# Delta mixer: turning the inverse back by blocks on VectorE instead of by TensorE transposes and ScalarE copies

## The chip, the cores and the metric

The kernel runs on one core of a Trainium2 chip. What counts is the device time of one execution in microseconds. Matrix products run on TensorE (PE in the profile, PEld its weight loads), elementwise work on VectorE (DVE), ScalarE (ACT) and GpSimd (POOL). Each engine works through its own list of instructions in order, and they are held together by semaphores.

## The reference

Four layers work on 2048 rows of 512 features, each adding to its input: a decay mixer, a feed-forward layer, the delta mixer and a second feed-forward layer. The change lies in the delta mixer alone. Its core, cut short:

```python
qkvz = hidden_states @ w_qkvz.T                     # 8 key heads, 16 value heads of 128
yc = silu(conv(q, k, v, 4 taps))                    # causal, per feature
beta, g = sigmoid(b), -exp(A_log) * softplus(a + dt_bias)
def step(S, xs):                                    # over the tokens
    qt, kt, vt, gt, bt = xs
    S = S * exp(gt)[..., None, None]
    delta = (vt - einsum('bhk,bhkv->bhv', kt, S)) * bt[..., None]
    S = S + einsum('bhk,bhv->bhkv', kt, delta)
    return S, einsum('bhk,bhkv->bhv', qt * scale, S)
out = (rmsnorm(o * silu(z)) * norm_weight) @ w_out.T
```

## The kernel before

The recurrence is computed in chunks of 128 tokens. Within a chunk the deltas solve a unit triangular system, and the kernel forms the inverse of its 128x128 matrix explicitly. There are 2 sequences of 8 chunks, 8 key heads and 2 value heads for each key head. One step handles one chunk of both sequences for one key head, so it has U = 4 matrices side by side, in tiles of 128 partitions x 4 x 128. Two such steps, the flights A and B, are worked on interleaved; together they are a pair. For each of 8 heads there are 4 pairs, so `pair` runs 32 times, most of it in hardware loops. Each engine has its own `pair`, which writes out by hand the order of its calls.

**The inverse.** `Tt` holds the transpose of the inverse, `T` the inverse itself, `At` the transposed matrix with its decays and signs. `unit_diagonal` on GpSimd presets `Tt` with the identity, and VectorE's `matrices` (L1586 to 1598) computes `At` and copies its 1-wide off-diagonal entries into `Tt` (L1597). Six levels i = 0 to 5 (`LV` = 6) then join diagonal blocks of 2, 4, ... 64 to blocks of twice the size. Before level i, `Tt` is nonzero only within diagonal blocks of 2, 4, 8, 16, 32 and 64 columns. In each level:

- `turn_back` (TensorE, L1825) transposes the four matrices of `Tt` into the PSUM bank `left`; at the last level only the upper left 64x64 of each.
- `turned` (ScalarE, L1322) copies what is needed of it into `T` (L1328, L1330, L1332).
- `level_x` (TensorE, L1838, "product x" below) multiplies `At` by `T` into `wide`; `level` (ScalarE, L1334) copies half of the result into `X` (L1339).
- `level_y` (TensorE, L1850, "product y") multiplies `X` by `Tt` into `right`; `level` (VectorE, L1600) copies the new blocks into `Tt` with a predicated copy (L1607), at the last level a plain one (L1604).

TensorE's f32 products of 128x128 are recorded as two instructions for each matrix, so one product x or y is x8.

**What lies between.** TensorE's order (L1925 to 1984) puts other products among the levels: `v` and `qk` (parts of the q, k, v projections of later pairs, `project`, L1782), `z` (halves of the z projection, L1795), `from_state` (L1869), `solve` (L1876). In the loop over levels one round is turn A, half a z, product y of B, product x of A, turn B, half a z, product y of A, product x of B; a half-step below is half of that. VectorE's order (L1678 to 1691) puts the convolutions of the next pair (`convolve`, L1526) behind the level copies, one or two behind each, and `right_side` (L1614) behind B's last predicated copy. ScalarE also squares the keys (`tokens`, L1311), which TensorE's `products` (L1821) waits for, and applies the first convolution taps. GpSimd splits the inputs of the pair after next in high and low parts (`split_x`, L1143 and 1147), once in four pairs the weights of the next head too (`low_weights`, L1158), and copies the input of the z projection (`plain_x`, L1153) when the last z is done.

**Semaphores.** `T` counts VectorE's writes of `Tt` (one for the start and one for each level), `Tps` the turns, `T0` the finished `T`, `px` and `py` the products, `X` the copies. `level_x` waits for `T0`, `turn_back` for `T` and at level 0 for `pt`.

Of the kernel before, what the change touches and what calls it, by code (L numbers as in the profile page):

```python
# [6 lines left out]
P = 128  # L7
# [959 lines left out]
def delta_mixer(nc, psum, consts, x_in, x_out, w):  # L967
# [21 lines left out]
    with ExitStack() as ctx:  # L989
# [43 lines left out]
        class Flight:  # L1033

            def __init__(self, g):
                self.i = g
                self.wide, self.left, self.right = bank[2 + 3 * g:5 + 3 * g]

                def buf(n, shape=(P, U, P)):
                    return sb(f"{n}{g}", list(shape))  # L1040

                self.here = slice(g * P, (g + 1) * P)
                self.qkv = buf("qkv", (P, 4, BATCH, P))
                self.z_raw, self.z_act = buf("z_raw"), buf("z_act")
                self.cur = buf("cur", (P, 5, U))
                (self.sr, self.ss, self.rr, self.brk, self.ncc, self.nr, self.rqs, self.q2, self.dcc, self.ssq, self.ssq_q,
                 self.ssq_eps, self.rn, self.rnq) = (
                    buf(n, (P, U)) for n in ("sr", "ss", "rr", "brk", "ncc", "nr", "rqs", "q2", "dcc", "ssq", "ssq_q",
                                             "ssq_eps", "rn", "rnq"))
                self.em, self.em_i = buf("em"), buf("em_i")  # L1050
                self.k_tok, self.rhs = buf("k_tok", (P, BATCH, P)), buf("rhs")
                self.d_end, self.At, self.Pt = (buf(n) for n in ("d_end", "At", "Pt"))
                self.d, self.junk = self.At, self.d_end
                self.T, self.Tt = buf("T"), buf("Tt")
                self.X, self.qs, self.o = self.em, self.T, self.T

                self.xf, self.xn, self.xnT = self.rhs, self.em, self.em_i
                self.s = {n: sem(f"{n}{g}") for n in (
                    "cur", "silu", "zact", "ss", "sse", "rr", "scal", "gU", "dt", "em", "emm",
                    "ktok", "vtok", "ktoks", "vtoks", "kqs", "qss", "at", "atm", "pt", "T0", "diag",  # L1060
                    "T", "Tps", "px", "X", "py", "rhs", "pd", "d", "pod", "dend", "ps", "o", "xf", "sqs",
                    "ssq", "sse2", "rn", "rnq", "xn", "txn", "xnT", "po", "acc")}

        flights = A, B = Flight(0), Flight(1)
# [2 lines left out]
            return b[:, :, :].rearrange("p u t -> p (u t)")  # L1067

        HP = P // 2

        def half(t, level, second):

# [165 lines left out]
        def _(act):  # L1238
# [80 lines left out]
                    act.activation(f.rhs[:, u, :], f.right[:, u, :], ACT.Copy, scale=f.nr[:, u // 2:u // 2 + 1]  # L1319
                                   ).then_inc(f.s["vtoks"], 1)  # L1320

            def turned(f, m, i):  # L1322
                act.wait_ge(f.s["Tps"], LV * m + i + 1)
                if i == 0:
                    act.wait_ge(f.s["xf"], m)
                act.wait_ge(f.s["px"], LV * m + i)
                if i == 0:
                    act.copy(f.T[:, :, :], f.left[:, :, :]).then_inc(f.s["T0"], 1)  # L1328
                elif i < LV - 1:
                    act.copy(half(f.T, i + 1, 0), half(f.left, i + 1, 0)).then_inc(f.s["T0"], 1)  # L1330
                else:
                    act.copy(f.T[0:HP, :, 0:HP], f.left[0:HP, :, 0:HP]).then_inc(f.s["T0"], 1)  # L1332

            def level(f, m, i):  # L1334
                act.wait_ge(f.s["px"], LV * m + i + 1)
                act.wait_ge(f.s["py"], LV * m + i)
# [34 lines left out]
            def pair(h, mm, first=False, start=False, over=False, turn=False, last=False, ahead=True):  # L1371
                m = h * PAIRS + mm
                decay(A, m)
                if not first:
                    output_T(B, m - 1)
                tokens(A, m)
                silu_qkv(B, m)
                silu_z(B, m)
                decay(B, m)
                values(A, m)  # L1380
                tokens(B, m)
                turned(A, m, 0)
                if not last:
                    copy_raw(2, m + 1)
                level(A, m, 0)
                if not last:
                    first_tap(0, m + 1)
                values(B, m)
                turned(A, m, 1)
                level(A, m, 1)  # L1390
                if not last:
                    first_tap(1, m + 1)
                turned(B, m, 0)
                level(B, m, 0)
                for i in range(2, LV):
                    turned(A, m, i)
                    if i == 2 and not last:
                        copy_raw(3, m + 1)
                        if over:
                            high_weights(h + 1)  # L1400
                    level(A, m, i)
                    turned(B, m, i - 1)
                    if 2 <= i <= 3 and not last:
                        first_tap(i, m + 1)
                    level(B, m, i - 1)
                    if i == 4 and not last:
                        copy_z(A, m + 1)
                from_state(A, m)
                turned(B, m, LV - 1)
                if not last:  # L1410
                    copy_z(B, m + 1)
                level(B, m, LV - 1)
                solved(A, m)
                if not last:
                    silu_qkv(A, m + 1)
                    silu_z(A, m + 1)
                mean_square(A, m)
                from_state(B, m)
                if ahead:
                    copy_raw(0, m + 2)  # L1420
                solved(B, m)
                output_T(A, m)
                mean_square(B, m)
                if ahead:
                    copy_raw(1, m + 2)
# [27 lines left out]
        def _(dve):  # L1453
# [132 lines left out]
            def matrices(f, m):  # L1586
                dve.wait_ge(f.s["em"], m + 1)
                dve.wait_ge(f.s["at"], m + 1)
                dve.wait_ge(f.s["scal"], NS * m + 4)
                dve.wait_ge(f.s["px"], LV * m)  # L1590
                for u in range(U):
                    dve.scalar_tensor_tensor(f.At[:, u, :], f.left[:, 2 * (u // 2) + 1, :], f.ncc[:, u:u + 1],
                                             f.em[:, u, :], ALU.mult, ALU.mult).then_inc(f.s["atm"], 1)
                dve.wait_ge(f.s["atm"], U * (m + 1))
                dve.wait_ge(f.s["diag"], m + 1)
                dve.sem_inc(s["dve_gate"], 1)
                dve.copy_predicated(half(f.Tt, 0, 1), first_part[:, :].rearrange("p (a n) -> p a n", n=1),  # L1597
                                    half(f.At, 0, 1)).then_inc(f.s["T"], 1)

            def level(f, m, i):  # L1600
                dve.wait_ge(f.s["py"], LV * m + i + 1)
                dve.wait_ge(f.s["T"], TN * m + 1 + i)
                if i == LV - 1:
                    dve.tensor_copy(f.Tt[0:HP, :, HP:P], f.right[0:HP, :, HP:P]).then_inc(f.s["T"], 1)  # L1604
                    return
                dve.sem_inc(s["dve_gate"], 1)
                dve.copy_predicated(half(f.Tt, i + 1, 1), new_part[:, i, :].rearrange("p (a n) -> p a n", n=LEVELS[i + 1]),  # L1607
                                    half(f.right, i + 1, 1)).then_inc(f.s["T"], 1)

            def right_side(f, m):  # L1610
                dve.wait_ge(f.s["kqs"], m + 1)
# [133 lines left out]
        def _(pe):  # L1745
# [76 lines left out]
                                   start=True, stop=True)  # L1822
                mm.then_inc(f.s["at"], 1)

            def turn_back(f, m, i):  # L1825
                if i == 0:
                    pe.wait_ge(f.s["pt"], m + 1)
                pe.wait_ge(f.s["T"], TN * m + 1 + i)
                if i == LV - 1:
                    pe.sem_inc(s["pe_gate"], 1)  # L1830
                for u in range(U):
                    if i < LV - 1:
                        mm = pe.transpose(f.left[:, u, :], f.Tt[:, u, :], ident[:, :])  # L1833
                    else:
                        mm = pe.transpose(f.left[0:HP, u, 0:HP], f.Tt[0:HP, u, 0:HP], ident[0:HP, 0:HP])
                mm.then_inc(f.s["Tps"], 1)

            def level_x(f, m, i):  # L1838
                pe.wait_ge(f.s["T0"], LV * m + i + 1)
                if i == LV - 1:  # L1840
# [68 lines left out]
            def pair(h, mm, first=False, start=False, over=False, turn=False, last=False, ahead=True):  # L1909
# [23 lines left out]
                decays(B, m)  # L1933
                tokens(B, m)
                v(0, HIGH)
                turn_back(A, m, 0)
                products(B, m)
                level_x(A, m, 0)
                v(1, [0])
                level_y(A, m, 0)  # L1940
                v(1, [1])
                turn_back(A, m, 1)
                v(1, [2])
                level_x(A, m, 1)
                v(1, [3])
                turn_back(B, m, 0)
                level_y(A, m, 1)
                level_x(B, m, 0)
                for i in range(2, LV):
                    f, b = flights[(i - 2) // 2], i % 2  # L1950
                    turn_back(A, m, i)
                    z(f, b, LOW)
                    level_y(B, m, i - 2)
                    level_x(A, m, i)
                    turn_back(B, m, i - 1)
                    z(f, b, HIGH)
                    level_y(A, m, i)
                    level_x(B, m, i - 1)
# [2 lines left out]
                from_state(A, m)  # L1961
                level_y(B, m, LV - 2)
                qk(0, 0)
                turn_back(B, m, LV - 1)
                qk(0, 1)
                solve(A, m)
                level_x(B, m, LV - 1)
# [114 lines left out]
```

## Time and profile before

| | |
|---|---|
| median of 3 runs | 3911.65 us (3900.70 to 3918.11) |
| span of the profiled execution | 3912.5 us (the page gives no other time of it) |
| mean granted TensorE clock | 0.973 |
| TensorE busy | 3615.0 us, 92% |
| VectorE busy | 2131.4 us, 54% |
| ScalarE busy | 1672.4 us, 43% |
| GpSimd busy | 827.5 us, 21% |

The profile is one execution, recorded by instruction. Busy times are shares over four layers with different limits, so a stage has to be looked at by itself. A row of the timeline gives start, duration, engine, line, what is written and read and how many instructions were merged, and in brackets how long the engine had been idle and what released it. A product's duration runs to its modelled end, past the start of the next one, since TensorE works them as a pipeline; what one occupies in the list is the distance to the next start.

### The profile page before, as it was taken

To read this page: it belongs to the slowest core of one execution; us is meant where nothing else is said; L and a number is where in the kernel's file an instruction comes from. 1 tells how busy PE (TensorE), PEld (TensorE's weight loads), DVE (VectorE), ACT (ScalarE), POOL (GpSimd) and SP (SyncE) were. 2 spreads that over 40 slices of the span, in tenths; PEclk is the share of its full clock that TensorE was granted. 3 is DMA by queue.
4 is the path that set the end of the run, shared out by engine and by line. 5 is a ranking of instruction groups with operands and counts; after the bars stand their busy time and mean duration, and the time that the engine had idled before them with its cause. 6 is when DMAs were issued, how large, how long until landed. Compare 5 with 4: busy or idle time off the path is not lost. (4 is left out here: it accounts for less than half of the span.)

```text
span 3912.5 us, 56006 instructions
## 1 busy us (share of the span) xinstructions
PE 3615.0 (92%) x19318; PEld 2817.6 (72%) x19318; DVE 2131.4 (54%) x4279; ACT 1672.4 (43%) x3964; POOL 827.5 (21%) x569
## 2 busy tenths in 40 slices
PE   5996999996899999999999999999999996899998
PEld 2444787884677878778778787787787875787787
DVE  6673555554555555555555555555555553455454
ACT  3343223221455455554554555545555453323221
POOL 1123002000423223223232232232222211201200
PEclk8998999998999999999999999999999998899999
DMA  4003102103000000000000000000000001211110
GB/s 157 11 32 119 43 32 97 65 22 105 11 1 7 17 2 7 17 2 7 18 1 7 18 1 6 18 6 2 18 7 6 12 12 55 76 64 65 65 54 33
DMA packets 61152, 126.88 MB, mean 32 GB/s; under 512 B 3008, under 2 KB 8384, under 8 KB 59840
## 3 DMA queue, kind: packets, MB, share of 16 engines
q1 hardware_dynamic: 60864, 123.26, 9.0%
q8 instruction: 154, 2.52, 0.3%
q14 instruction: 134, 1.10, 0.1%
HBM read 98.09 MB, written 25.17 MB: 32 GB/s over the span
## 5 line engine op out<-in xcount | busy, mean ns | idle before, releaser
L1607 DVE COPY_PREDICATED b_Tt<-b_new_part,banks 128x256 f32<-128x256 uint8 x320 | 157.6, 493 | 557.8 <-PE banks L1858 557.8
L895 PE MATMUL banks<-f_x_hi,f_w_hi 128*128 128x512 f32 x1024 | 408.4, 399 | 43.1 <-ACT f_silu L764 23.7
L895 PE MATMUL banks<-f_x_lo,f_w_hi 128*128 128x512 f32 x1024 | 406.0, 397 | 0.0
L895 PE MATMUL banks<-f_x_hi,f_w_lo 128*128 128x512 f32 x1024 | 405.8, 396 | 0.0
L1526 DVE SCALAR_TENSOR_TENSOR b_conv<-b_raw,b_taps,b_conv 128x512 f32<-128x512 f32 x384 | 376.2, 999 | 2.9 <-ACT b_conv L1279 2.6
L1339 ACT COPY b_em<-banks 128x256 f32<-128x256 f32 x320 | 120.5, 376 | 545.0 <-PE banks L1844 545.0
L1858 PEld LDWEIGHTS banks<-b_Tt,b_em 128*128 128x128 f32 x2560 | 331.5, 192 | 23.9 <-issue 9.6
L1844 PE MATMUL banks<-b_T,b_At 128*128 128x128 f32 x2560 | 347.5, 279 | 0.5 <-ACT b_T L1330 0.5
L1858 PE MATMUL banks<-b_Tt,b_em 128*128 128x128 f32 x2560 | 341.4, 276 | 0.9 <-ACT b_em L1339 0.6
L830 DVE TENSOR_TENSOR f_h<-banks,f_silu 128x512 f32<-128x512 f32 x128 | 87.1, 689 | 435.6 <-PE banks L895 358.8
L1844 PEld LDWEIGHTS banks<-b_T,b_At 128*128 128x128 f32 x2560 | 313.4, 193 | 14.7 <-ACT b_T L1330 7.0
L1795 PE MATMUL banks<-b_w_z,b_x_cur 128*128 128x256 f32 x1024 | 265.4, 383 | 0.0
L895 PEld LDWEIGHTS banks<-f_x_hi,f_w_hi 128*128 128x128 f32 x1024 | 196.9, 192 | 90.8 <-ACT f_silu L764 26.3
L1782 PE MATMUL banks<-b_x_hi,b_w_hi 128*128 128x512 f32 x512 | 253.0, 494 | 9.0 <-POOL b_w_lo L1158 6.0
L1906 PE MATMUL banks<-b_o_cur,b_em_i 128*128 128x512 f32 x512 | 239.7, 612 | 20.5 <-ACT b_em_i L1368 17.6
L1833 PE MATMUL banks<-b_ident,b_Tt 128*128 128x128 f32 x1280 | 203.6, 282 | 35.3 <-DVE b_Tt L1597 16.5
L895 PEld LDWEIGHTS banks<-f_x_hi,f_w_lo 128*128 128x128 f32 x1024 | 196.8, 192 | 42.2
L895 PEld LDWEIGHTS banks<-f_x_lo,f_w_hi 128*128 128x128 f32 x1024 | 197.0, 192 | 41.5
L764 ACT ACTIVATE f_silu<-banks 128x512 f32<-128x512 f32 x128 | 76.2, 597 | 323.8 <-PE banks L895 323.8
L925 PE MATMUL banks<-f_w_hi,f_k_hi 128*128 128x512 f32 x512 | 204.8, 400 | 6.6 <-DVE f_k_lo L852 6.6
L1782 PE MATMUL banks<-b_x_hi,b_w_lo 128*128 128x512 f32 x512 | 203.9, 398 | 0.0
L925 PE MATMUL banks<-f_w_hi,f_k_lo 128*128 128x512 f32 x512 | 203.2, 397 | 0.0
(264 smaller groups left out, 7229.2 us busy)
## 6 DMA issues: line engine op xcount, KB each, us to landing
f_x_tok<-rows SPq DMA_DIRECT2D x16, 1024.0 KB, 7.5
f_stage<-in_ffn_gate SPq DMA_DIRECT2D x8, 1024.0 KB, 6.8
f_stage<-in_ffn_up SPq DMA_DIRECT2D x8, 1024.0 KB, 8.5
f_stage<-in_ffn_down SPq DMA_DIRECT2D x8, 1024.0 KB, 4.9
f_x_res<-rows SPq DMA_DIRECT2D x8, 1024.0 KB, 5.6
f_part<-f_x_res SPq DMA_DIRECT2D x8, 1024.0 KB, 4.3
f_x_res<-f_part SPq DMA_DIRECT2D x8, 1024.0 KB, 5.6
b_w_load<-in_b_qkvz SPq DMA_DIRECT2D x8, 1024.0 KB, 6.1
```

Of the source, the lines that this page charges most:

```text
L830: dve.tensor_tensor(h[:, r, :], up_ps[:, r % 2, :], silu[:, r % 2, :], ALU.mult).then_inc(s_h, 1)
L895: mm = pe.matmul(bank, w[:, b, kind, cols], x[:, k, :], start=(k == 0 and i == 0), stop=(k == KD - 1 and i == 2))
L925: mm = pe.matmul(out_ps[i // 2][:, i % 2, :], k[:, r, toks], w[:, b, DOWN, r * D:(r + 1) * D], start=(b == 0 and r == 0 and j == 0), stop= ...
L1339: act.copy(half(f.X, i + 1, 0), half(f.wide, i + 1, 0)).then_inc(f.s["X"], 1)
L1526: dve.scalar_tensor_tensor(conv[:, i, :, :], raw[:, i, :, tap:tap + 2 * P], taps[:, i, tap:tap + 1], conv[:, i, :, :], ALU.mult, ALU.add). ...
L1607: dve.copy_predicated(half(f.Tt, i + 1, 1), new_part[:, i, :].rearrange("p (a n) -> p a n", n=LEVELS[i + 1]), half(f.right, i + 1, 1)).the ...
L1782: mm = pe.matmul(flat(bank[i % 2]), wt[:, k, i * P:(i + 1) * P], xt[:, k, :, :].rearrange("p b t -> p (b t)"), start=(k == 0 and wt is w_h ...
L1795: mm = pe.matmul(bank[f.i][:, 2 * b:2 * b + 2, :], x_cur[:, k, b, f.here], w_z[:, k, :], start=(k == 0), stop=(k == KD - 1))
L1833: mm = pe.transpose(f.left[:, u, :], f.Tt[:, u, :], ident[:, :])
L1844: mm = pe.matmul(f.wide[:, u, :], f.At[:, u, :], f.T[:, u, :], start=True, stop=True)
L1858: mm = pe.matmul(f.right[:, u, :], f.X[:, u, :], f.Tt[:, u, :], start=True, stop=True)
L1906: mm = pe.matmul(out, f.xnT[:, 2 * b + i, :], o_cur[:, i, :], start=(i == 0), stop=(i == 1))
```

## The change

`T` is no longer made by TensorE and ScalarE. VectorE transposes `Tt` into `T` with its own transpose, which turns each 32x32 block in its place; up to blocks of 32 that is the whole transpose, as all nonzero entries lie within diagonal blocks. At the last level the one new 32x32 block of the upper left 64x64 is transposed to its mirrored place, while the rest of `T` stands from the level before. The transpose follows at once behind the copy that it reads, in `matrices` and in `level`, and signals `T0`. `turn_back`, ScalarE's `turned` and the semaphore `Tps` are dropped, the order of all other calls is kept.

```diff
 # VectorE, behind the first copy in matrices
+                turned(f, m, 0)
+
+            def turned(f, m, i):
+                dve.wait_ge(f.s["T"], TN * m + 1 + i)
+                if i < LV - 1:
+                    dve.transpose(flat(f.T), flat(f.Tt)).then_inc(f.s["T0"], 1)
+                else:
+                    dve.transpose(f.T[QP:HP, :, 0:QP], f.Tt[0:QP, :, QP:HP]).then_inc(f.s["T0"], 1)
 # VectorE, at the end of level (not at the last level)
                 dve.copy_predicated(half(f.Tt, i + 1, 1), new_part[:, i, :]..., half(f.right, i + 1, 1)).then_inc(f.s["T"], 1)
+                turned(f, m, i + 1)
 # ScalarE
-            def turned(f, m, i):
-                act.wait_ge(f.s["Tps"], LV * m + i + 1)
...
-                if i == 0:
-                    act.copy(f.T[:, :, :], f.left[:, :, :]).then_inc(f.s["T0"], 1)
-                elif i < LV - 1:
-                    act.copy(half(f.T, i + 1, 0), half(f.left, i + 1, 0)).then_inc(f.s["T0"], 1)
-                else:
-                    act.copy(f.T[0:HP, :, 0:HP], f.left[0:HP, :, 0:HP]).then_inc(f.s["T0"], 1)
 # TensorE
-            def turn_back(f, m, i):
...
-                for u in range(U):
-                    if i < LV - 1:
-                        mm = pe.transpose(f.left[:, u, :], f.Tt[:, u, :], ident[:, :])
-                    else:
-                        mm = pe.transpose(f.left[0:HP, u, 0:HP], f.Tt[0:HP, u, 0:HP], ident[0:HP, 0:HP])
-                mm.then_inc(f.s["Tps"], 1)
 # TensorE, in pair (six such calls for each flight go, and six of ScalarE's)
                 for i in range(2, LV):
-                    turn_back(A, m, i)
                     z(f, b, LOW)
                     level_y(B, m, i - 2)
                     level_x(A, m, i)
-                    turn_back(B, m, i - 1)
                     z(f, b, HIGH)
                     level_y(A, m, i)
                     level_x(B, m, i - 1)
```

`HP` is 64, `QP` 32, `TN` 7.

## Rows read from the trace of the kernel before

**Rows 1.** Windows view, one pair: busy us of PE, PEld, DVE, ACT, POOL; then PEclk

```profile
2248.66:2318.99 70.33, 68.44 (x430) 54.98 (x429) 38.75 (x91) 37.17 (x105) 17.71 (x15) 1.00 0.00 1
```

**Rows 2.** The line that starts an inverse: its instructions (min/median/max ns)

```profile
L1597 DVE COPY_PREDICATED b_Tt<-b_first_part,b_At x64: 731/743/1164, 1039.4 to 3248.0; 128x256 f32<-128x256 uint8 x64
```

**Rows 3.** Groups by line: count, busy us, mean ns, idle before and its releasers

```profile
L1833 PE MATMUL banks<-b_ident,b_Tt 128*128 128x128 f32 x1280 | 203.6, 282 | 35.3 <-DVE b_Tt L1597 16.5 <-DVE b_Tt L1607 11.4
...
L1835 PE MATMUL banks<-b_ident,b_Tt 64*64 64x64 f32 x256 | 25.2, 218 | 3.6 <-DVE b_Tt L1607 1.5
...
L1339 ACT COPY b_em<-banks 128x256 f32<-128x256 f32 x320 | 120.5, 376 | 545.0 <-PE banks L1844 545.0
```

**Rows 4.** Timeline of TensorE in the levels of that pair (start us, duration us)

```profile
2266.91 0.66 PE L1833 MATMUL banks<-b_ident,b_Tt 128*128 128x128 f32 x4
...
2267.40 1.03 PE L1795 MATMUL banks<-b_w_z,b_x_cur 128*128 128x256 f32 x4
2268.26 1.05 PE L1858 MATMUL banks<-b_Tt,b_em 128*128 128x128 f32 x8
2269.15 1.06 PE L1844 MATMUL banks<-b_T,b_At 128*128 128x128 f32 x8
...
2270.05 0.60 PE L1833 MATMUL banks<-b_ident,b_Tt 128*128 128x128 f32 x4
```

**Rows 5.** Groups by line: VectorE on 128x512 f32, one and two SBUF sources

```profile
L1474 DVE TENSOR_SCALAR b_x_cur<-b_acc,b_mean,b_rstd 128x512 f32<-128x512 f32 x16 | 7.7, 542 | 15.8 <-PE banks L1753 12.7 <-POOL b_rstd L1137 3.1
...
L1654 DVE TENSOR_TENSOR b_em<-b_rhs,b_rnq 128x512 f32<-128x512 f32 x64 | 44.2, 691 | 2.2
```

**Rows 6.** Timeline, start of the inverses of that pair, all engines

```profile
2248.66 1.13 DVE L1597 COPY_PREDICATED b_Tt<-b_first_part,b_At 128x256 f32<-128x256 uint8 x1 [0.18 <-DVE b_At L1592]
...
2249.85 0.66 PE L1833 MATMUL banks<-b_ident,b_Tt 128*128 128x128 f32 x4 [0.47 <-DVE b_Tt L1597]
2249.89 0.27 ACT L1311 ACTIVATION_READ_ACCUMULATOR b_d_end<-banks 128x1 f32 x1
...
2250.34 1.07 PE L1821 MATMUL banks<-b_qkv 128*128 128x256 f32 x4
...
2252.90 1.13 PE L1858 MATMUL banks<-b_Tt,b_em 128*128 128x128 f32 x8
...
2254.29 0.73 DVE L1607 COPY_PREDICATED b_Tt<-b_new_part,banks 128x256 f32<-128x256 uint8 x1 [2.02 <-PE banks L1858]
...
2256.75 0.74 DVE L1597 COPY_PREDICATED b_Tt<-b_first_part,b_At 128x256 f32<-128x256 uint8 x1 [0.19 <-DVE b_At L1592]
...
2259.21 1.10 PE L1844 MATMUL banks<-b_T,b_At 128*128 128x128 f32 x8
```

**Rows 7.** Timeline, VectorE and GpSimd in the middle of that pair's levels

```profile
2260.28 5.68 POOL L1147 TENSOR_TENSOR b_x_lo<-b_xT,b_x_hi 128x512 fp32r<-128x512 f32 x4 [0.18 <-POOL b_x_hi L1143]
...
2263.24 3.27 DVE L1526 SCALAR_TENSOR_TENSOR b_conv<-b_raw,b_taps,b_conv 128x512 f32<-128x512 f32 x2
...
2266.76 0.74 DVE L1526 SCALAR_TENSOR_TENSOR b_conv<-b_raw,b_taps,b_conv 128x512 f32<-128x512 f32 x1
```

**Rows 8.** Timeline, end of the inverses of that pair, all engines

```profile
2284.17 1.89 POOL L1153 COPY b_x_cur<-b_xT 128x2048 f32<-128x2048 f32 x1 [18.21 <-PE banks L1795]
...
2285.53 1.89 PE L1869 MATMUL banks<-b_state,b_qkv 128*128 128x256 f32 x8
...
2288.49 0.45 DVE L1607 COPY_PREDICATED b_Tt<-b_new_part,banks 128x256 f32<-128x256 uint8 x1 [1.89 <-PE banks L1858]
...
2288.83 1.12 DVE L1614 SCALAR_TENSOR_TENSOR b_rhs<-banks,b_cur,b_rhs 128x128 f32<-128x128 f32 x4
...
2290.20 1.05 PE L1876 MATMUL banks<-b_rhs,b_Tt 128*128 128x128 f32 x8
```

**Rows 9.** First pair: granted clock in a stretch (PEclk), and TensorE's timeline

```profile
1040.00:1050.00 10.00, 8.15 (x41) 6.78 (x42) 4.22 (x15) 5.43 (x21) 2.08 (x2) 0.83 0.01 2
...
1042.21 1.72 PE L1821 MATMUL banks<-b_qkv 128*128 128x256 f32 x4 [1.33 <-ACT b_d_end L1311]
```

More of the change, by code:

```diff
@@ L1060, in __init__ @@
                     "ktok", "vtok", "ktoks", "vtoks", "kqs", "qss", "at", "atm", "pt", "T0", "diag",
-                    "T", "Tps", "px", "X", "py", "rhs", "pd", "d", "pod", "dend", "ps", "o", "xf", "sqs",
+                    "T", "px", "X", "py", "rhs", "pd", "d", "pod", "dend", "ps", "o", "xf", "sqs",
                     "ssq", "sse2", "rn", "rnq", "xn", "txn", "xnT", "po", "acc")}
@@ L1069, in delta_mixer @@
         HP = P // 2
+        QP = P // 4
         def half(t, level, second):
@@ L1320, in values @@
                                    ).then_inc(f.s["vtoks"], 1)
-            def turned(f, m, i):
-                act.wait_ge(f.s["Tps"], LV * m + i + 1)
-                if i == 0:
-                    act.wait_ge(f.s["xf"], m)
-                act.wait_ge(f.s["px"], LV * m + i)
-                if i == 0:
-                    act.copy(f.T[:, :, :], f.left[:, :, :]).then_inc(f.s["T0"], 1)
-                elif i < LV - 1:
-                    act.copy(half(f.T, i + 1, 0), half(f.left, i + 1, 0)).then_inc(f.s["T0"], 1)
-                else:
-                    act.copy(f.T[0:HP, :, 0:HP], f.left[0:HP, :, 0:HP]).then_inc(f.s["T0"], 1)
             def level(f, m, i):
@@ L1381, in pair @@
                 tokens(B, m)
-                turned(A, m, 0)
                 if not last:
@@ L1388, in pair @@
                 values(B, m)
-                turned(A, m, 1)
                 level(A, m, 1)
@@ L1392, in pair @@
                     first_tap(1, m + 1)
-                turned(B, m, 0)
                 level(B, m, 0)
                 for i in range(2, LV):
-                    turned(A, m, i)
                     if i == 2 and not last:
@@ L1401, in pair @@
                     level(A, m, i)
-                    turned(B, m, i - 1)
                     if 2 <= i <= 3 and not last:
@@ L1408, in pair @@
                 from_state(A, m)
-                turned(B, m, LV - 1)
                 if not last:
@@ L1823, in products @@
                 mm.then_inc(f.s["at"], 1)
-            def turn_back(f, m, i):
[L1826 to L1830, printed above, removed]
-                for u in range(U):
-                    if i < LV - 1:
-                        mm = pe.transpose(f.left[:, u, :], f.Tt[:, u, :], ident[:, :])
-                    else:
-                        mm = pe.transpose(f.left[0:HP, u, 0:HP], f.Tt[0:HP, u, 0:HP], ident[0:HP, 0:HP])
-                mm.then_inc(f.s["Tps"], 1)
             def level_x(f, m, i):
@@ L1935, in pair @@
                 v(0, HIGH)
-                turn_back(A, m, 0)
                 products(B, m)
@@ L1941, in pair @@
                 v(1, [1])
-                turn_back(A, m, 1)
                 v(1, [2])
@@ L1945, in pair @@
                 v(1, [3])
-                turn_back(B, m, 0)
                 level_y(A, m, 1)
@@ L1963, in pair @@
                 qk(0, 0)
-                turn_back(B, m, LV - 1)
                 qk(0, 1)
```

## The prediction

> **What bounds the kernel now.** I read the engine table first, then busy time over one pair of chunks, then the timelines of that pair. The loop over pairs runs 32 times, two inverses each [rows 2], from 1039 to some 3270 us, so 2.2 ms of the 3.91 ms lie there. One pair is 70.33 us from one start of flight A's inverse to the next, and TensorE is busy in 68.44 of it, at granted clock 1.00, while VectorE is busy in 38.75 and ScalarE in 37.17 [rows 1]. So TensorE's instruction list sets the pace, and time taken out of it shortens the pair, as long as nothing else arrives later. VectorE's 55% is an average: the inverse levels hold its convolutions and its half of the chain at once, so they have to be walked through.
>
> **What is removed.** Per pair and flight five turns of four 128x128 transposes and one of four 64x64. In all, 1280 and 256 instructions, busy 203.6 and 25.2 us, 7.15 us per pair [rows 3]. What a turn costs in the list is its start to the next start, 0.49 us (2266.91 to 2267.40) [rows 4]; ten of them and two small ones at 0.30 (by the ratio of their busy times) are 5.5 us per pair. The waits just before them, 35.3 + 3.6 us in all [rows 3], 1.2 us per pair, are waits for VectorE and go only if VectorE is earlier. The twelve ScalarE copies also go. I cost them at nothing: ScalarE is half idle. What they leave behind is that product x now has only the z projection, 0.86 us [rows 4], between itself and product y, which needs ScalarE's copy of x: x drains 0.16 us past the next start (1.06 against 0.90), the copy takes 0.38 [rows 3], two hand-offs about 0.15; 0.69 fits in 0.86. If a ScalarE convolution tap lay in front it wouldn't, but these are queued right behind the preceding copy.
>
> **What is added.** Ten VectorE transposes of 128x512 f32 per pair and two of 32x128, each waiting for the copy just ahead of it on the same engine. No transpose of VectorE is in this trace. Bounds for the large one: 0.542 us, an operation with one source on the same shape, and 1.38, twice the 0.691 of one with two sources, should four-byte elements take two passes [rows 5]. I take 0.70, nearest to the 0.691 row, because the operation has to carry 512 elements per partition through the engine once. The small one lies between a quarter of 0.542, as it has a quarter of the columns, and the 0.45 of a copy with twice as many [rows 5, 8]; I take 0.25. What queues behind a transpose: the convolutions, then in turn the other flight's matrices, its level copy, and flight A's right side.
>
> The Trainium skill speaks against the move for whole matrices: "VectorE: DVE Perf Modes", section "The three transpose paths", gives TensorE for a full 128x128, and 311 ns for a VectorE transpose of 128x128 bf16, 32x32 blocks only. If all of that grew with the columns, an estimate from that page is 4 x 311 = 1.24 us here, and the sum would land at the tipping point worked out below (no gain). No run here shows it.
>
> **Walk through the pair with 0.70 us**, against the times of before; copies, products and convolutions keep their measured times.
>
> Start of the inverses [rows 6]. A's first copy ends at 2249.79, transpose to 2250.5. TensorE no longer stops for the turn, but the next product waits for ScalarE's last square, which ends at 2250.16: it starts about 2250.25 instead of 2250.34. Only 0.1 gained, as half a microsecond of the turn was cover for ScalarE. Product y of A's first level starts at 2252.8, and its copy (0.26 us behind y's end, as 2254.03 to 2254.29) ends at 2254.93. Then comes the new transpose to 2255.67, and only then B's matrices. Before, from that copy's start to the end of B's first copy (2254.29 to 2257.49) it took 3.20; now it takes 3.20 + 0.74 (transpose and its wait) from 2254.2, to 2258.1, and B's own transpose lasts to 2258.9. Product x of B starts at 2259.0 to 2259.1 against 2259.21. **So three turns went (1.5 us) and 0.1 to 0.2 us is won**: VectorE's chain is the later one here.
>
> Levels [rows 4, 7]. From there TensorE's half-step is z + y + x, 0.86 + 0.89 + 0.90 = 2.65, instead of 3.14 with the turn. VectorE has to do copy 0.45, transpose 0.74 with its wait, and one or two convolutions of 0.74: 1.9 or 2.7, so it just keeps up. But while GpSimd splits the inputs (2260.28 to 2265.96), two convolutions take 3.27 instead of 1.5. There VectorE falls behind: A's third level copy starts about 2266.2, its transpose ends at 2267.4, and TensorE stands about 0.4. After that product x follows every 2.65.
>
> End [rows 8]. The last z projection now ends about 4 us earlier, GpSimd's input copy (1.89 us) follows at once and slows one convolution to about 1.6 (by rows 7) just ahead of A's last copy. The product with the state starts at 2282.4 instead of 2285.53, 3.1 us earlier. B's level copy is followed by the small transpose, 0.25, before A's right side (2288.83 in before, ready for the solve at 2290.20), so the solve starts 2.9 us earlier. TensorE idles 0.8 ahead of it, so B's last turn brings nothing. Behind the solve the order is as before.
>
> A pair thus gains 2.9 us of 5.5. In the eight pairs where GpSimd also splits the next head's weights, three more convolutions are slowed by 0.89 each, 2.7, of which two half-steps with slack of 0.75 take up 1.5; 1.2 is left, and the gain is 1.7. Sum: 24 x 2.9 + 8 x 1.7 = 83 us. The profiled span is 3912.5, 0.9 us from the median of 3911.65, so both serve as base. **3912 - 83 = 3829 us.**
>
> **Rivals.**
> - *GpSimd also slows the transposes*, as it does the convolutions (3.27 for two, 2.2 times) [rows 7]. Three transposes fall there; 0.84 us more each leaves TensorE standing 1.1 longer, three more such in the eight pairs cost another 2.5: 24 x 1.8 - 8 x 1.9 = 28 us, **3884**. For: every slowed convolution overlaps GpSimd. Against: the convolution has two tensors in SBUF, the transpose one. In the Trainium skill, "SBUF — State Buffer", section "Who interferes with whom" says that a VectorE instruction with at most one SBUF input, outside the two-port modes, doesn't contend with GpSimd; by that this rival falls, and the row agrees so far as the slowed one has two. 12%.
> - *The clock drops.* TensorE will stand 1.0 + 0.5 + 0.9 us in the 10 us around 2249 to 2259. In the first pair, where it stood like that (1.33 us before 1042.21), the clock was 0.83 over 10 us, a mean of its two levels 1.2 and 2.4 GHz, and a product took 1.72 instead of 1.07 [rows 6, 9]. Two to three such products cost about 1.7 per pair: 83 - 54 = 29, **3883**. Against: clock 1.00 over the whole pair now [rows 1], waits of 0.47 included. 10%.
> - *VectorE is never late* (transposes near 0.54, the convolutions move out of GpSimd's way): the 5.5 us go in full, 176 us, **3736**. 8%.
> - *VectorE takes the bound without price or gain*: transpose of 1.0 to 1.25, within 20 us of **3905**. 7%.
> - *Slower: the transpose takes two passes*, 1.38 us. Two of them stand ahead of B's first product x: 1.3 us late. Then VectorE never rests until A's last copy: 8 copies, 3.9; 7 x 1.38 + 0.25 of transposes; 11 convolutions at 0.70, pipelined; four of them slowed, 3.6; waits 0.8: 25.9 us from 2260.5 to 2286.4. With that copy and a hand-off, 0.5, the state's product starts at 2286.9 against 2285.53, 1.4 late, and the solve 1.6; in the eight 2.7 more. 24 x 1.6 + 8 x 4.3 = 73: **3985**. Each 0.1 us of the transpose is worth 0.9 us of a pair there, so this decides from about 1.2 us on. For: four-byte data and no row. Against: the rows of this shape in SBUF that GpSimd doesn't slow are at 0.74 or under [rows 5, 7]. 11%.
>
> **How the numbers follow.** The forecast has 52%. Below 0.70 us for the transpose the pair gains up to 0.8 us more (3800), so its own range is 3795 to 3850. The range of 8 in 10 takes in the slowed transposes and the clock and half the way to the full gain, and leaves out the two-pass case and most of the 7%: 3770 to 3900. A measurement of this kernel can tell about 0.5%, 20 us: faster 52 + 12 + 10 + 8 = 82%; within it 8% and slower 10%, as a hundredth of the two-pass case may end near the tipping point.
>
> **What would show it.** Right: pair near 67.4 us; the transpose at 0.65 to 0.75; TensorE waiting for VectorE's transposes ahead of x of B's first level, about 0.9 us, and ahead of A's solve; half-steps of 2.65 after GpSimd's split; VectorE busy 46 us of a pair. Wrong: a transpose over 1 us, or one that is longer beside GpSimd; a granted clock under 1.00 inside a pair; the product y waiting for ScalarE; a gain already at the first x of B.

## The result and the profile after

| | before | after |
|---|---|---|
| median | 3910.73 us (4 runs) | 3847.08 us (3845.45 to 3852.50, 4 runs) |
| span of the profiled execution | 3912.5 us | 3843.7 us |
| ratio | | 0.9842, 95% interval 0.9825 to 0.9858 |
| mean granted TensorE clock | 0.973 | 0.973 |

The changed kernel is 64 us faster, 1.6%. 3829 us was forecast, 83 us less, within 3770 to 3900. Of the runs further down, one of the four of the kernel with each transpose twice was slow (5033.58 us at a granted clock of 0.65), and that kernel's time is the median of the other three. The lines of the kernel after are numbered anew: product x is L1823, product y L1837, the small product x L1825, the product with the state L1848, A's and B's solve L1855, the transposes L1587 and L1589, the first copy L1580, the level copies L1598 and L1595, the right side L1606.

The windows view of the same pair of chunks, from one first copy of flight A to the next (stretch, its length, then busy us of PE, PEld, DVE, ACT, POOL, then the granted clock):

```profile
2214.64:2282.91 68.27, 63.42 (x382) 50.33 (x381) 48.00 (x103) 32.34 (x93) 17.98 (x15) 1.00 0.00 1
```

The answer to [rows 1]: the pair lasts 68.27 us instead of 70.33. TensorE gave up 5.0 us of busy time (68.44 to 63.42) and only 2.06 became time; it now rests 4.9 us of a pair. VectorE went from 38.75 to 48.00, and the clock stayed at 1.00. The new operations in the groups by line (count, busy us, mean ns, idle before):

```profile
L1587 DVE STREAM_TRANSPOSE b_T<-b_Tt 128x512 f32<-128x512 f32 x320 | 227.7, 711 | 11.0
...
L1589 DVE STREAM_TRANSPOSE b_T<-b_Tt 32x128 f32<-32x128 f32 x64 | 19.3, 301 | 2.2
```

The large transpose takes 0.711 us (0.70 was taken), the small one 0.301 (0.25 was taken).

The new waits of TensorE within the loop (us in total, times, longest):

```profile
PE banks L1855 <- DVE b_rhs L1606: 45.0, 63, 2.2
PE banks L1848 <- DVE b_Tt L1595: 39.4, 30, 1.4
PE banks L1823 <- DVE b_T L1587: 36.0, 93, 1.7
PE banks L1813 <- ACT b_d_end L1312: 33.9, 33, 2.3
```

Of these, 18.0 us of the first row and 2.6 of the last were there before, and the third row stands in the place of 27.9 us (16.5 and 11.4) that the turns waited for VectorE's copies [rows 3]. The rest came with the change: ahead of the solve, of the product with the state, of product x, and of the product behind ScalarE's squares. They show up in the timeline of the pair, first at the start of the inverses (start us, duration us):

```profile
2216.23 1.10 PE L1813 MATMUL banks<-b_qkv 128*128 128x256 f32 x4 [0.86 <-ACT b_d_end L1312]
...
2220.88 0.71 DVE L1587 STREAM_TRANSPOSE b_T<-b_Tt 128x512 f32<-128x512 f32 x1
...
2221.65 1.16 PE L1823 MATMUL banks<-b_T,b_At 128*128 128x128 f32 x8 [0.35 <-DVE b_T L1587]
...
2223.34 1.10 PE L1837 MATMUL banks<-b_Tt,b_em 128*128 128x128 f32 x8
...
2223.39 0.74 DVE L1580 COPY_PREDICATED b_Tt<-b_first_part,b_At 128x256 f32<-128x256 uint8 x1 [0.19 <-DVE b_At L1575]
...
2224.16 0.71 DVE L1587 STREAM_TRANSPOSE b_T<-b_Tt 128x512 f32<-128x512 f32 x1
...
2224.93 1.16 PE L1823 MATMUL banks<-b_T,b_At 128*128 128x128 f32 x8 [0.49 <-DVE b_T L1587]
```

To set these against [rows 6], add 34.02 us, by which the pair starts earlier. The product behind the squares (2216.23, so 2250.25) now waits 0.86 for them, and B's first product x (2224.93, so 2258.95 against 2259.21) waits for the transpose behind B's first copy. A's second transpose (2220.88) stands ahead of B's matrices. Then the levels and the end, to be set against [rows 7] and [rows 8]:

```profile
2232.65 0.71 DVE L1587 STREAM_TRANSPOSE b_T<-b_Tt 128x512 f32<-128x512 f32 x1
...
2233.42 1.16 PE L1823 MATMUL banks<-b_T,b_At 128*128 128x128 f32 x8 [0.28 <-DVE b_T L1587]
...
2245.56 3.00 DVE L1509 SCALAR_TENSOR_TENSOR b_conv<-b_raw,b_taps,b_conv 128x512 f32<-128x512 f32 x2
...
2246.12 1.90 POOL L1154 COPY b_x_cur<-b_xT 128x2048 f32<-128x2048 f32 x1 [14.39 <-PE banks L1787]
...
2248.49 0.41 DVE L1595 COPY b_Tt<-banks 64x256 f32<-64x256 f32 x1
...
2248.95 1.99 PE L1848 MATMUL banks<-b_state,b_qkv 128*128 128x256 f32 x8 [1.30 <-DVE b_Tt L1595]
...
2252.50 0.30 DVE L1589 STREAM_TRANSPOSE b_T<-b_Tt 32x128 f32<-32x128 f32 x1
...
2252.84 1.12 DVE L1606 SCALAR_TENSOR_TENSOR b_rhs<-banks,b_cur,b_rhs 128x128 f32<-128x128 f32 x4
...
2254.01 1.16 PE L1855 MATMUL banks<-b_rhs,b_Tt 128*128 128x128 f32 x8 [0.78 <-DVE b_rhs L1606]
```

Once in the levels (2233.42) TensorE stands 0.28 for a transpose (2232.65) behind slowed convolutions. Then two convolutions take 3.00 us beside GpSimd's copy at 2246.12, A's last copy comes behind them at 2248.49, and the product with the state waits 1.30 for it. The solve waits 0.78 for a right side that stands behind B's level copy and the small transpose.

### The profile page after: what moved, and what is told of

The parts are those of the page before. It is cut to its first block and busy times, and to the rows that moved or that the text cites. A ratio compares the mean times of both kernels' runs of the same rounds, so it can differ in the third digit from the quotient of the medians.

```text
span 3843.7 us, 52310 instructions
## 1 busy us (share of the span) xinstructions
PE 3451.3 (90%) x17782; PEld 2666.1 (69%) x17782; DVE 2413.0 (63%) x4663; ACT 1519.6 (40%) x3580; POOL 841.6 (22%) x569
## 5 line engine op out<-in xcount | busy, mean ns | idle before, releaser
L1509 DVE SCALAR_TENSOR_TENSOR b_conv<-b_raw,b_taps,b_conv 128x512 f32<-128x512 f32 x384 | 404.0, 1072 | 3.9 <-ACT b_conv L1280 2.6
L1823 PE MATMUL banks<-b_T,b_At 128*128 128x128 f32 x2560 | 353.4, 281 | 36.0 <-DVE b_T L1587 36.0
L1823 PEld LDWEIGHTS banks<-b_T,b_At 128*128 128x128 f32 x2560 | 315.7, 193 | 64.9 <-DVE b_T L1587 61.0
L1837 PEld LDWEIGHTS banks<-b_Tt,b_em 128*128 128x128 f32 x2560 | 330.5, 192 | 35.0 <-ACT b_em L1328 11.0
L1837 PE MATMUL banks<-b_Tt,b_em 128*128 128x128 f32 x2560 | 342.6, 277 | 4.4 <-ACT b_em L1328 4.4
L1598 DVE COPY_PREDICATED b_Tt<-b_new_part,banks 128x256 f32<-128x256 uint8 x320 | 156.8, 490 | 242.4 <-PE banks L1837 239.1
L1587 DVE STREAM_TRANSPOSE b_T<-b_Tt 128x512 f32<-128x512 f32 x320 | 227.7, 711 | 11.0
L925 PE MATMUL banks<-f_w_lo,f_k_hi 128*128 128x512 f32 x512 | 203.3, 397 | 0.0
```

What stands on the lines that cost most here:

```text
L925: mm = pe.matmul(out_ps[i // 2][:, i % 2, :], k[:, r, toks], w[:, b, DOWN, r * D:(r + 1) * D], start=(b == 0 and r == 0 and j == 0), stop= ...
L1509: dve.scalar_tensor_tensor(conv[:, i, :, :], raw[:, i, :, tap:tap + 2 * P], taps[:, i, tap:tap + 1], conv[:, i, :, :], ALU.mult, ALU.add). ...
L1587: dve.transpose(flat(f.T), flat(f.Tt)).then_inc(f.s["T0"], 1)
L1823: mm = pe.matmul(f.wide[:, u, :], f.At[:, u, :], f.T[:, u, :], start=True, stop=True)
L1837: mm = pe.matmul(f.right[:, u, :], f.X[:, u, :], f.Tt[:, u, :], start=True, stop=True)
```

## The experiments

The theory after the result: TensorE's list no longer sets the end at three places of a pair, where VectorE's queue is the later one: ahead of B's first product x, ahead of the product with the state (with GpSimd's copy beside the convolutions), and ahead of A's solve. The rivals: TensorE's list alone counts, at 0.49 us a turn, or the gain is spread evenly over the turns. The ratios below are against the kernel before on the same chip, whose median there was 3908.7 to 3910.8 us; microseconds over or under the changed kernel are counted from its 3847.08, taken beside 3910.73.

**Each large transpose twice.**

```diff
                 if i < LV - 1:
+                    dve.transpose(flat(f.T), flat(f.Tt)).then_inc(f.s["twice"], 1)
+                    dve.wait_ge(f.s["twice"], (LV - 1) * m + i + 1)
                     dve.transpose(flat(f.T), flat(f.Tt)).then_inc(f.s["T0"], 1)
```

> The changed kernel, with each of the ten large VectorE transposes of a pair done twice, one waiting for the other (0.71 + 0.04 + 0.71 = 1.46 us); the output is the same. Theory (VectorE's chain sets the end at the start of the inverses, and has only some 3.2 us of rest in the levels): 1.5 us later at the first product x of B, 5.3 us more in the levels of which 3.2 were rest, so 3.6 us a pair over the changed kernel, 3962 us, slower than the kernel before. Rival (TensorE's list sets the pace and VectorE has room, being busy 67% of a pair): under 1 us a pair, 3847 to 3880 us.

3968.0 us (3963.18 to 3978.47, 3 runs), ratio 1.014 (1.012 to 1.016), 121 us over the changed kernel where 115 were worked out. The waits of TensorE (product x, product with the state, solve):

```profile
PE banks L1825 <- DVE b_T L1589: 94.3, 101, 2.5
PE banks L1850 <- DVE b_Tt L1597: 59.5, 31, 2.1
PE banks L1857 <- DVE b_rhs L1608: 41.7, 62, 2.2
```

and the windows view of the pair that answers to the one above (columns as there; the pairs of this kernel's loop last from 71.1 to 75.4 us):

```profile
2285.83:2356.95 71.12, 64.03 (x382) 50.40 (x381) 53.18 (x114) 32.33 (x93) 17.50 (x15) 1.00 0.00 1
```

TensorE's busy time is that of the changed kernel (64.03 against 63.42), but it waits 94.3 us for the transposes instead of 36.0 and 59.5 instead of 39.4 ahead of the product with the state. VectorE is busy in 75% of the pair and yet sets the end: an engine well short of full can be the bound by its place in the chain.

Not all of the 121 us is VectorE's, though. The pair shown is one of 7 among 31 in which the granted clock stayed at 1.00. In the other 24 its mean was lower, mostly 0.98. Here are one of these, a stretch of it, and the product with the state that falls there:

```profile
1404.63:1477.17 72.54, 65.44 (x382) 51.43 (x381) 53.16 (x114) 32.32 (x93) 17.49 (x15) 0.98 0.00 1
...
1441.50:1444.60 3.10, 2.82 (x7) 2.28 (x8) 0.89 (x2) 0.00 (x0) 0.00 (x0) 0.50 0.00 0
...
1441.78 3.41 PE L1850 MATMUL banks<-b_state,b_qkv 128*128 128x256 f32 x8 [1.97 <-DVE b_Tt L1597]
```

TensorE stood 1.97 us, the granted clock in that stretch was 0.50, the lower of its two levels (1.2 and 2.4 GHz), and the product took 3.41 us where it takes 1.99 at 1.00. In the pair shown first TensorE stood 1.96 us at the same place and the clock stayed up; what decides between the two is not shown. So at 1.00 a pair like the one shown is 2.85 us longer than in the changed kernel, and the one with the weights' split that stayed at 1.00 is 4.3 longer (72.52 against 68.25), some 3.2 in the mean where 3.6 were worked out; the lower clock added some 1.4 us (72.54 against 71.12) to most of the others. That the total came near the 115 is in part luck. At 71.12 us the pair is still longer than the 70.33 of the kernel before. The forecast's slower rival had the right mechanism; its premise, a transpose of 1.38 us, is not what the chip does.

**Only the first turn of each flight on VectorE.** The five later turns go the old way.

```diff
                                     half(f.At, 0, 1)).then_inc(f.s["T"], 1)
+                blocks(f, m, 0)                          # the transpose on VectorE
 # TensorE's turn_back and ScalarE's turned
+                if i in BLOCKS:                          # BLOCKS = (0,)
+                    return
```

> The kernel before, with only the first turn of each flight (the one behind the first copy) done by VectorE; the five later turns of each flight stay with TensorE and ScalarE. Theory (ahead of the levels nothing is won, as TensorE then waits for ScalarE's squares and for VectorE): -0.2 to +0.2 us a pair, 3904 to 3917 us. Rival 1 (the gain is spread over the turns): two of twelve turns, 2 of 12 of 64 us, 3900 us. Rival 2 (TensorE's list alone counts): two turns of 0.49 a pair, 31 us, 3880 us.

3885.06 us, ratio 0.9937 (0.9920 to 0.9953): 26 us less, where the theory had none and the list alone 31. The theory fell here. The transpose of B, product y of A and product x of B in the timeline of the pair that starts at 2237.33:

```profile
2246.09 0.71 DVE L1611 STREAM_TRANSPOSE b_T<-b_Tt 128x512 f32<-128x512 f32 x1
...
2246.46 1.08 PE L1876 MATMUL banks<-b_Tt,b_em 128*128 128x128 f32 x8
...
2247.38 1.06 PE L1862 MATMUL banks<-b_T,b_At 128*128 128x128 f32 x8
```

B's transpose ends at 2246.8, before TensorE is through with product y, so product x follows at once, 10.05 us into the pair instead of 10.55 [rows 6]: the whole 0.49 of B's turn is won. And as everything then lies half a microsecond earlier, TensorE's short wait in the levels goes too; the product with the state is 0.77 us earlier. So it isn't true that the turns ahead of the levels are worth nothing. What takes their worth back in the changed kernel is A's *second* transpose (0.71 us), which there stands between A's level copy and B's matrices, in the chain to B's product x.

**Only the five later turns on VectorE** (`BLOCKS = (1, 2, 3, 4, 5)` in the same kernel).

> The changed kernel, with the first turn of each flight given back to TensorE and ScalarE; the five later ones stay on VectorE. Theory: B's first turn through TensorE and ScalarE ends 0.6 us later than the transpose, so 0.3 to 0.6 us a pair over the changed kernel, 3857 to 3866 us; the whole gain over the kernel before lies in the later turns. Rival 1 (spread evenly): 10 of 12 of 64 us, 3858 us. Rival 2 (TensorE's list alone): 1.0 us a pair over the changed kernel, 3878 us.

3872.48 us, ratio 0.9903 (0.9887 to 0.9920), 25 us over the changed kernel, where the theory had 10 to 19 and the list alone 31. TensorE's first turn of B, product y of A and product x of B, in the pair that starts at 2225.86, and a later product x of the next pair, in which GpSimd splits the weights:

```profile
2235.65 0.63 PE L1851 MATMUL banks<-b_ident,b_Tt 128*128 128x128 f32 x4 [0.75 <-DVE b_Tt L1602]
2236.12 1.06 PE L1876 MATMUL banks<-b_Tt,b_em 128*128 128x128 f32 x8
2237.01 1.10 PE L1862 MATMUL banks<-b_T,b_At 128*128 128x128 f32 x8
...
2314.67 1.16 PE L1862 MATMUL banks<-b_T,b_At 128*128 128x128 f32 x8 [0.86 <-DVE b_T L1611]
```

B's turn waits 0.75 us for VectorE, and product y of A, which was ready, is queued behind it: it starts 10.26 us into the pair instead of 8.70 in the changed kernel. I had counted the turn's length but not who stands behind its wait. Product x of B is 0.86 us late by it, but the wait of 0.28 in the levels then goes, and the pair ends up only 0.4 longer (68.65 against 68.27), as the theory had it. What it missed are the pairs with the weights' split: there product x waits 0.86 for a transpose behind slowed convolutions (2314.67) instead of 0.30, and they are 1.3 us longer or more (69.51 at the least against 68.20 to 68.25). The two halves, 26 and 38 us, add up to the 64 of the change.

**GpSimd's copy held back.**

```diff
             def plain_x(q, c):
                 pool.wait_ge(s["pz"], 2 * q)
+                pool.wait_ge(s_conv[3], 3 * q)
```

> The changed kernel, with GpSimd's copy of the z projection's input held back until the convolutions of the pair are done (one more wait; it is needed only in the next pair). Theory (this copy, now earlier beside two convolutions, costs them 3.00 instead of 1.4 us just ahead of A's last copy, and TensorE 1.30 us ahead of the product with the state): the two convolutions at 1.4 us, the product with the state 1.0 to 1.3 us earlier, 32 to 42 us less, 3805 to 3815 us. Rival (the queue of VectorE is as long without it, or the next wait takes its place at once): 3840 to 3847 us.

3799.41 us, ratio 0.9717 (0.9700 to 0.9733), 48 us less than the changed kernel for one added wait, more than the 32 to 42 expected. The end of the inverses, in the pair that starts at 2187.29:

```profile
2218.18 1.38 DVE L1510 SCALAR_TENSOR_TENSOR b_conv<-b_raw,b_taps,b_conv 128x512 f32<-128x512 f32 x2
...
2219.47 0.41 DVE L1596 COPY b_Tt<-banks 64x256 f32<-64x256 f32 x1
...
2220.11 1.89 PE L1849 MATMUL banks<-b_state,b_qkv 128*128 128x256 f32 x8
...
2220.71 1.89 POOL L1155 COPY b_x_cur<-b_xT 128x2048 f32<-128x2048 f32 x1 [16.36 <-DVE b_conv L1510]
```

The two convolutions take 1.38 us instead of 3.00, A's last copy follows, and the product with the state starts without a wait, 32.82 us into the pair instead of 34.31. That is the 1.5 us of a pair that was won. The copy now runs behind the convolutions, where nobody waits for it.

**The same wait in the kernel before.**

> The kernel before, with GpSimd's copy of the z projection's input held back in the same way as in the run on the changed kernel that gained 48 us. Theory (there the copy fell beside one convolution behind A's last copy, with VectorE resting 1.89 us afterwards): no change, 3903 to 3916 us. Rival (the copy costs that kernel as much, and the gain has nothing to do with the change): 3863 to 3880 us.

3907.11 us, ratio 0.9996 (0.9987 to 1.0006): nothing. The convolutions' group by line shows that they got faster all the same:

```profile
L1527 DVE SCALAR_TENSOR_TENSOR b_conv<-b_raw,b_taps,b_conv 128x512 f32<-128x512 f32 x384 | 351.9, 936 | 2.9 <-ACT b_conv L1280 2.6
```

936 ns instead of 999 in the mean, 24 us of VectorE's time less, but there VectorE rested behind them. So GpSimd's copy cost nothing before and 48 us after: the change moved it onto the path.

**B's matrices ahead of A's first level copy.** The first copy into `Tt` and its transpose become a function of their own (`start_inverse`).

```diff
-                level(A, m, 0)
                 within_chunk(B, m)
                 matrices(B, m)
+                level(A, m, 0)
+                start_inverse(B, m)
```

> The changed kernel, with VectorE doing the mask product and the four matrices of flight B ahead of A's first level copy, where it rested 1.56 us, and only B's first copy and transpose behind it. Theory (A's second transpose stands in the chain of B's start; alone it is that order that keeps B's first product x waiting 0.49 us): that product 0.5 to 0.7 us earlier in each pair, 16 to 22 us less, 3825 to 3831 us. Rival (the later waits, ahead of the product with the state and the solve, swallow it): 3842 to 3850 us.

3820.31 us, ratio 0.9781 (0.9763 to 0.9799), 27 us less than the changed kernel, some more than the 16 to 22 expected. B's transpose and product x, in the pair that starts at 2199.78, and a later product x of the next pair, in which GpSimd splits the weights:

```profile
2207.38 0.71 DVE L1589 STREAM_TRANSPOSE b_T<-b_Tt 128x512 f32<-128x512 f32 x1
...
2209.41 1.06 PE L1827 MATMUL banks<-b_T,b_At 128*128 128x128 f32 x8
...
2285.67 1.16 PE L1827 MATMUL banks<-b_T,b_At 128*128 128x128 f32 x8 [1.02 <-DVE b_T L1589]
```

Product x of B starts 9.63 us into the pair instead of 10.29, without a wait. In two pairs of four the period fell from 68.3 to 67.1, more than the 0.66 won there, as the wait of 0.28 in the levels went too: behind it TensorE's list is 1.2 us earlier. Where GpSimd splits the weights the period stayed at 68.2: at that place product x waits 1.02 us (2285.67) and gives all of it back. In the first pair of seven heads it is 69.8 to 71.0, each at a granted clock of 0.98, where the changed kernel has 70.6 to 70.9 in three at 1.00 and 71.0 to 72.3 in four at 0.98.

**A's right side first.**

```diff
                     for f in flights:
+                        if (i, f.i) == (LV - 1, 1):
+                            right_side(A, m)
                         level(f, m, i - f.i)
...
-                right_side(A, m)
```

> The changed kernel, with A's right side (four operations, 1.12 us) ahead of B's level copy and small transpose on VectorE, not behind them. Theory (TensorE waits 0.78 us ahead of A's solve because the right side stands behind that copy and transpose, while VectorE rested before them): the wait goes, 0.7 to 0.85 us a pair, 3820 to 3825 us. Rival (B's copy is then late, and its last level or the solve of B takes the wait over): 3840 to 3850 us.

3813.01 us, ratio 0.9760 (0.9743 to 0.9776), 34 us less than the changed kernel, more than the 22 to 27 expected. The right side and the solve, in the pair that starts at 2199.65:

```profile
2236.05 1.13 DVE L1606 SCALAR_TENSOR_TENSOR b_rhs<-banks,b_cur,b_rhs 128x128 f32<-128x128 f32 x4 [1.43 <-PE banks L1849]
...
2238.12 1.05 PE L1856 MATMUL banks<-b_rhs,b_Tt 128*128 128x128 f32 x8
```

VectorE starts the right side as soon as the product with the state is there, and the solve waits for nothing: 38.47 us into the pair instead of 39.37.

**All three.**

> The changed kernel with all three: GpSimd's copy held back, B's matrices early, A's right side first. Theory (three separate waits): the sum of the single gains, 48 + 16 to 22 + 22 to 27, 3750 to 3761 us. Rival (they share one chain): no better than 3785 us.

3738.91 us, ratio 0.9566 (0.9550 to 0.9582). 108 us less than the changed kernel, 109 being the sum of the single gains as measured (the 3750 to 3761 expected still had two of them smaller): the three waits were separate, and this kernel beats both the one before and the changed one. What is left of TensorE's waits (the squares, product x, the solve of B):

```profile
PE banks L1819 <- ACT b_d_end L1313: 33.9, 33, 2.4
PE banks L1829 <- DVE b_T L1590: 23.1, 43, 1.7
PE banks L1861 <- DVE b_rhs L1609: 17.2, 32, 1.2
```

The wait ahead of the product with the state is gone, and the solve's is back at what it was before the change.

**The three edits on the kernel before.**

> The kernel before with the same three edits of order (GpSimd's copy held back, B's matrices early, A's right side first). Theory (these waits came with the change; the kernel before hardly has them, TensorE standing only 0.3 to 0.5 us at three places of a pair, none of which the edits touch): 3895 to 3912 us, so that the change is worth some 4% once the order fits it. Rival (the order alone is worth the 108 us): 3800 to 3820 us.

3905.62 us, ratio 0.9990 (0.9980 to 0.9999): as good as nothing. The order is worth 3 us without the change and 108 with it.

**ScalarE's squares first**, on top of all three.

```diff
                 decay(B, m)
-                values(A, m)
                 tokens(B, m)
+                values(A, m)
```

> The kernel with all three edits, and on ScalarE the squares of B's keys ahead of A's four value copies, so that TensorE doesn't wait 0.9 us for them ahead of its product. Theory (the next in line is VectorE's chain of scales, matrices and copies, hardly earlier): the wait at the product goes, B's first product x is at most 0.3 us earlier, 3728 to 3740 us. Rival (ScalarE's squares set the start of the inverses): 0.6 to 0.85 us a pair, 3711 to 3720 us.

3736.22 us, ratio 0.9558 (0.9542 to 0.9574), not to be told from the kernel with all three. The waits of product x and of the product behind the squares:

```profile
PE banks L1829 <- DVE b_T L1590: 46.5, 74, 2.3
...
PE banks L1819 <- ACT b_d_end L1313: 3.9, 3, 1.3
```

The wait for the squares falls from 33.9 to 3.9 us and the wait of product x rises from 23.1 to 46.5: it was handed on to VectorE, as the theory said.

## Why the prediction was right, and where it wasn't

- **What bounds the kernel.** Right: TensorE's list set the pace, and a pair got shorter. The forecast share, 2.9 us of 5.5, was too good; it is 2.06.
- **The price of the transpose.** 0.70 us taken, 0.711 measured, and the same in all instances. That it came out near the 0.691 row and not near the 0.542 one is in part luck: the reason given, 512 elements a partition once through the engine, holds for both rows.
- **Start of the inverses.** Worked out: the product behind the squares at 2250.25, product y at 2252.8, B's product x at 2259.0 to 2259.1. Measured, with the 34.02 added: 2250.25, 2252.81 and 2258.95. TensorE's three waits there, 1.0, 0.5 and 0.9 in the forecast, are 0.86, 0.35 and 0.49. The sum was right, the reading of it wasn't: B's transpose is worth the 0.5 us of its turn, and A's second transpose costs it again, as the second and the sixth experiment show.
- **Levels.** Worked out: A's third level copy at 2266.2, its transpose to 2267.4, TensorE standing 0.4. Measured: 2266.22, 2267.38 and 0.28. Half-steps of 2.65 as forecast.
- **End of the inverses.** This term was mis-sized. I had GpSimd's copy slow one convolution to 1.6 us; it slowed two to 3.00, so the product with the state came at 2282.97 instead of 2282.4, and with the small transpose at 0.30 the solve at 2288.03 instead of 2287.3. Behind the solve 0.1 us more was lost than before; what takes it was not followed up. Of 24 pairs each lost 0.85 us of the forecast that way, 20 us.
- **The pairs with the weights' split.** The loop has seven, not eight: of the eight heads' splits the first stands ahead of it. 1.7 us was worked out, but they gained as much as the others, 2.1: their period is 68.2. The extra slowing of three convolutions was wrong: in the pair behind the one shown, the three that fall beside the weights' split take 0.71 us and 2.39 for two, against 1.43 and 2.94 before, and GpSimd's split takes 6.86 instead of 6.31. That the delay moved from VectorE to GpSimd is my reading; no run tested it.
- **Rivals.** GpSimd doesn't slow the transposes, see the last section. The clock stayed at 1.00 in the pair, in spite of 0.86 + 0.35 + 0.49 us of standing at the start; over the run it was lower in 5 of 31 pairs, against 4 before. The rival isn't empty: with each transpose twice it was lower in 24. VectorE as the bound is real: at 1.46 us a transpose the kernel is slower than before, as that rival had it from 1.2 on; the point itself was not measured. "VectorE is never late" (5.5 us a pair) was off by more than half.

The 64 us are thus 5.0 us of TensorE's busy time a pair less 3 us of new waits; the forecast knew all three waits and had the one with GpSimd's copy too small.

## What to carry to other kernels

A step moved from the bound engine to one that rests half of the time is worth what is left after a walk through that engine's queue: look for what stands right behind each new operation, not at the busy share. Then mend the order: here three small edits of order, worth 3 us in the kernel before, brought 108 us after the move, from 1.6% to 4.3%. And ask which transfers and copies of other engines start earlier now, and beside what they will run.

## What the runs showed of the hardware

The large blockwise transpose has a nearly fixed time, in all 320 instances (min/median/max ns):

```profile
L1587 DVE STREAM_TRANSPOSE b_T<-b_Tt x320: 711/711/715, 1039.3 to 3206.4; 128x512 f32<-128x512 f32 x160
```

By 0.711 us for 512 columns on 128 partitions and 0.301 for 128 columns on 32, an estimate is 1.07 ns a column and 0.16 us besides, if the number of partitions makes no difference, which no run tested. The Trainium skill's 311 ns for 128x128 in bf16 ("VectorE: DVE Perf Modes", "The three transpose paths") lies near the small one, though no run here has that type, and four times that, 1.24 us, was not the price of four times the columns.

Transposes ran beside GpSimd's splits without getting longer, while the convolutions behind them got longer:

```profile
2225.86 5.87 POOL L1148 TENSOR_TENSOR b_x_lo<-b_xT,b_x_hi 128x512 fp32r<-128x512 f32 x4 [0.18 <-POOL b_x_hi L1144]
...
2228.79 0.71 DVE L1587 STREAM_TRANSPOSE b_T<-b_Tt 128x512 f32<-128x512 f32 x1
2229.43 2.85 DVE L1509 SCALAR_TENSOR_TENSOR b_conv<-b_raw,b_taps,b_conv 128x512 f32<-128x512 f32 x2
```

By the start and end times of the trace, 81 of the 320 large transposes lie wholly within GpSimd's splits and its copies of the inputs, and none took over 0.715 us. The two convolutions right behind the one shown took 2.85 instead of 1.4. The convolution reads two tensors from SBUF, the transpose one. That agrees with what the Trainium skill says in "SBUF — State Buffer", "Who interferes with whom": a VectorE instruction with at most one SBUF input, outside the two-port modes, doesn't contend with GpSimd. Which mode the transpose runs in no trace shows.
